# A Flamingo gated layer on one core: the query projection as three float32r products of high and low parts

## The reference

```python
h   = layernorm(x)
Q   = heads(h   @ Wq.T + bq)          # 16 heads of 16
K,V = heads(ctx @ Wk.T + bk), heads(ctx @ Wv.T + bv)
E   = where(mask == 0, -1e10, Q K^T / sqrt(16))
x   = x + tanh(g_xattn) * (softmax(E) V @ Wfc.T + bfc)
g   = layernorm(x) @ gate             # 8 experts, the best 2 with softmax weights
x   = x + tanh(g_ffn) * sum over the 2 of  w * ((silu(h w0_e) * (h w1_e)) wo_e)
```

## Time and profile before

| what | us |
|---|---|
| median of 3 runs | 1440.11 |
| lowest and highest run | 1439.74, 1444.11 |
| the profiled execution, span | 1441.3 |
| attention stage in it, about | 0 to 740 |
| expert stage in it, about | 750 to 1441 |

### The profile page before, as it was taken

How to read it: one execution, slowest core, us unless ns; L and a number is a source line. 1 busy time by engine, 2 the same in 40 slices (tenths; PEclk the granted TensorE clock), 3 DMA queues, 4 the chain that set the end, 5 groups by cost and what they waited for, 6 DMA issues and landing times.

```text
span 1441.3 us, 35541 instructions
## 1 busy us (share of the span) xinstructions
PE 1340.0 (93%) x9634; PEld 1173.3 (81%) x9635; DVE 808.2 (56%) x2519; ACT 697.4 (48%) x1779; POOL 895.5 (62%) x1389
## 2 busy tenths in 40 slices
PE   3999999999999999999939999999999999999996
PEld 3898888888888888888827788888888888888885
DVE  3688788888788888888643333333333333333332
ACT  2566566566566566566513333333333333333332
POOL 3478888888888888888853344444444444444443
PEclk9999999999999999999959999999999999999998
DMA  5033313333313333313677784333333333333332
GB/s 148 18 112 120 119 58 108 123 118 115 117 61 108 123 118 115 117 61 108 205 209 211 200 220 80 54 51 55 54 51 58 52 51 54 55 51 52 58 52 38
DMA packets 73811, 139.70 MB, mean 97 GB/s; under 512 B 11568, under 2 KB 54992, under 8 KB 71600
## 3 DMA queue, kind: packets, MB, share of 16 engines
q0 software_dynamic: 32064, 52.46, 18.5%
q1 hardware_dynamic: 39696, 84.87, 18.2%
q10 hardware_dynamic: 2016, 1.93, 0.5%
HBM read 68.95 MB, written 70.27 MB: 97 GB/s over the span
## 4 chain that ended last, share of the span: by engine, by line
PE 53%; issue 13%; POOL 11%; DVE 10%; DMA 6%; ACT 5%; POOLq 1%; DVEq 1%; ACTq 0%; SPq 0%; another core or an unknown queue 0%
PE banks L1296 23%; PE psB L1315 12%; PE banks L1137 4%; PE psT L1304 3%; DMA out_dram<-ey,eid 3%; POOL routed_rows L478 2%; DMA et<-routed_rows 2%; PE psG L1281 2%; ACT prob L604 2%; PE psT L1149 2%; PE banks L1089 2%; ACT prob L608 2%; DVE qT L809 2%; PE psB L1161 1%; POOL rs L421 1%
## 5 line engine op out<-in xcount | busy, mean ns | idle before, releaser
L531 POOL DMA_INDIRECT out_dram<-ey,eid x135 | 217.3, 1609 | 374.8 <-issue 141.0
L1296 PE MATMUL banks<-w_all,etT 128*128 x1620 | 434.2, 403 | 0.7 <-ACT etT L715 0.7
L1038 DVE TENSOR_TENSOR hgT<-psT,hgT 128x512 fp32r<-128x512 f32 x135 | 93.4, 692 | 430.4 <-ACT hgT L727 430.4
L1296 PEld LDWEIGHTS banks<-w_all,etT 128*128 128x128 f32 x1620 | 287.0, 190 | 51.4 <-issue 3.4
L1315 PEld LDWEIGHTS psB<-w_all,hgT 128*128 128x128 f32 x1620 | 208.1, 188 | 17.9 <-issue 1.3
L1315 PE MATMUL psB<-w_all,hgT 128*128 x1620 | 216.9, 283 | 0.8 <-ACT hgT L727 0.8
L733 ACT ACTIVATE ey<-psB,ewt 128x256 f32<-128x256 f32 x135 | 64.1, 475 | 240.4 <-DMA out_dram<-ey,eid 180.1
L721 ACT ACTIVATE hs<-banks 128x512 f32<-128x512 f32 x135 | 80.7, 598 | 186.1 <-PE psT L1304 181.5
L432 POOL TENSOR_TENSOR kbd<-kT,own 128x616 fp32r<-128x616 f32 x128 | 152.4, 1222 | 24.3 <-DVE kT L831 24.3
L1161 PE MATMUL psB<-vbd,probT 128*128 128x51 f32 x1280 | 160.0, 273 | 0.0
L1161 PEld LDWEIGHTS psB<-vbd,probT 128*128 128x128 f32 x1280 | 157.2, 194 | 1.6
(11 more groups left out here) (159 smaller groups left out, 2309.3 us busy)
## 6 DMA issues: line engine op xcount, KB each, us to landing
split_weights<-w_part SPq DMA_DIRECT2D x16, 1536.0 KB
w_all<-split_weights SPq DMA_DIRECT2D x32, 768.0 KB
et<-routed_rows POOLq DMA_DIRECT2D x135, 129.0 KB, 3.3
xb<-in_x_dram SPq DMA_DIRECT2D x32, 256.0 KB, 2.8
w_raw<-in_L_ffn_w_kernel_dram SPq DMA_DIRECT2D x32, 256.0 KB
out_dram<-x SPq DMA_DIRECT2D x64, 128.0 KB
w_raw<-in_L_ffn_wo_kernel_dram SPq DMA_DIRECT2D x16, 256.0 KB
cb<-in_ctx_dram SPq DMA_DIRECT2D x32, 77.0 KB
```

The source lines that it names most:

```text
L531: gp.indirect_dma_start(out=out, out_offset=bass.IndirectOffsetOnAxis(ap=eid[:, u:u + 1], axis=0), in_=ey[:, u % 2, :], in_offset=None, co ...
L1296: m = pe.matmul(banks4[:, bank], etT[:, u % 2, a, c], weight(e, c, w, n), start=(j == 0), stop=(j == len(steps) - 1))
```

## The change

Both operands of the query projection are held as a high and a low part in float32r. The two high parts are what ACT's copies write (of the weights once, of x in each batch); the two low parts are new subtractions on DVE, `psum - high`: one for the weights at the start, and `x_low(b)` for each batch, 128 x 512 elements each. `queries` then makes three products of parts (high x high, low weights x high x, high weights x low x) in float32r where there was one in float32. PE waits for the low part of x (`xT_lo`) ahead of each `queries`, and for that of the weights (`wq_lo`) before it does anything behind the weights' transposes.

```diff
--- before.py
+++ after.py
@@ -100,7 +100,7 @@
         sb("early_weights", [P, EARLY * 2 * QW])
         w_raw = sb("w_raw", [P, FR, F])
         w_part = sb("w_part", [P, 2, FR, F], F32R)
-        wT = {n: sb(f"{n}T", [P, DC, D]) for n in ("wk", "wq", "wv", "wfc")}
+        wT = {n: sb(f"{n}T", [P, DC, D]) for n in ("wk", "wv", "wfc")}
         gate_sb = sb("gate_sb", [P, DC, E])
         bias = sb("bias", [P, 3, DC])
         bfc_rows = sb("bfc_rows", [P, D])
@@ -134,7 +134,8 @@
         xg = sb("xg", [P, 2, QT, D])
         cb = sb("cb", [K2, 2, D])
         xn = sb("xn", [P, QT, D])
-        xnT = sb("xnT", [P, DC, S])
+        xnT = sb("xnT", [P, 2, DC, S], F32R)
+        wqT = sb("wqT", [P, 2, DC, D], F32R)
         ctxT = sb("ctxT", [P, DC, K2])
         vparts = sb("vparts", [K2, 3, D], BF16)
         vrest = sb("vrest", [K2, D])
@@ -221,7 +222,7 @@
         x1_out, pad_out, scattered = [sem("x1_out0"), sem("x1_out1")], sem("pad_out"), [sem(f"scattered{j}") for j in range(4)]
 
         iota_done, ident_done, dv_const = sem("iota_done"), sem("ident_done"), sem("dv_const")
-        wT_ps, wT_sb, tanh_done, valid_done = sem("wT_ps"), sem("wT_sb"), sem("tanh_done"), sem("valid_done")
+        wT_ps, wT_sb, wq_lo, xT_lo, tanh_done, valid_done = sem("wT_ps"), sem("wT_sb"), sem("wq_lo"), sem("xT_lo"), sem("tanh_done"), sem("valid_done")
 
         stat1, mvar1, eps1, rstd1, xn_done = sem("stat1"), sem("mvar1"), sem("eps1"), sem("rstd1"), sem("xn_done")
         xg_done, kbd_done, mrow_done = sem("xg_done"), sem("kbd_done"), sem("mrow_done")
@@ -564,9 +565,10 @@
                         act.dma_start(bias[:, n, a:a + 1], v[a * P:(a + 1) * P].rearrange("(q o) -> q o", o=1)).then_inc(const_in, 16)
             act.wait_ge(gates_in, 32)
             act.activation(tanhg[:], gates[:], ACT.Tanh).then_inc(tanh_done, 1)
-            for n, name in enumerate(wT):
+            for n, name in enumerate(("wk", "wq", "wv", "wfc")):
                 act.wait_ge(wT_ps, n + 1)
-                act.copy(wT[name][:].rearrange("p c d -> p (c d)"), banks4[:, n]).then_inc(wT_sb, 1)
+                dst = wqT[:, 0] if name == "wq" else wT[name][:]
+                act.copy(dst.rearrange("p c d -> p (c d)"), banks4[:, n]).then_inc(wT_sb, 1)
             act.wait_ge(const_in, 16 * CONST_LOADS)
 
             def ctx_evac(b):
@@ -584,7 +586,7 @@
 
             def x_evac(b):
                 act.wait_ge(xT_ps, b + 1)
-                act.copy(xnT[:].rearrange("p c s -> p (c s)"), psA[:]).then_inc(xT_sb, 1)
+                act.copy(xnT[:, 0].rearrange("p c s -> p (c s)"), psA[:]).then_inc(xT_sb, 1)
 
             def q_evac(b, u):
                 act.wait_ge(q_ps, b + 1)
@@ -808,6 +810,11 @@
 
                 return dve.scalar_tensor_tensor(out=dst, in0=ps_part, scalar=bias_part, in1=high.bitcast(F32), op0=ALU.add, op1=ALU.subtract)
 
+            def x_low(b):
+                dve.wait_ge(xT_sb, b + 1)
+                dve.tensor_tensor(xnT[:, 1].rearrange("p c s -> p (c s)"), psA[:], xnT[:, 0].rearrange("p c s -> p (c s)").bitcast(F32),
+                                  ALU.subtract).then_inc(xT_lo, 1)
+
             def q_low(b, u):
                 dve.wait_ge(q_sb, DC * (b + 1))
                 for a in range(DC):
@@ -925,6 +932,10 @@
                 dve.tensor_copy(slot[:, u4], slotf[:]).then_inc(slot_done, 1)
                 dve.wait_ge(base_done, i + 1)
 
+            dve.wait_ge(wT_sb, 2)
+            dve.tensor_tensor(wqT[:, 1].rearrange("p c d -> p (c d)"), banks4[:, 1], wqT[:, 0].rearrange("p c d -> p (c d)").bitcast(F32),
+                              ALU.subtract).then_inc(wq_lo, 1)
+            x_low(0)
             k_evac(0)
             k_split(0, 0)
             k_split(0, 1)
@@ -937,6 +948,7 @@
             s_negate(0, 0)
             s_shift(0, 0)
             k_evac(1)
+            x_low(1)
             k_split(1, 0)
             k_split(1, 1)
 
@@ -986,6 +998,8 @@
                         place(i - 3, (u4 - 3) % 4)
                     if known(i, 2):
                         choose(i - 2)
+                    if t == 1 and more2:
+                        x_low(b + 2)
 
             batches(dve, batch)
             free_rows(NT - 3, 0)
@@ -1101,8 +1115,10 @@
             def queries(b, a):
 
                 pe.wait_ge(xT_sb, b + 1)
-                for c in range(DC):
-                    m = pe.matmul(psA[:, a * S:(a + 1) * S], wT["wq"][:, c, a * P:(a + 1) * P], xnT[:, c], start=(c == 0), stop=(c == DC - 1))
+                pe.wait_ge(xT_lo, b + 1)
+                for j, (w, x_part) in enumerate(((0, 0), (1, 0), (0, 1))):
+                    for c in range(DC):
+                        m = pe.matmul(psA[:, a * S:(a + 1) * S], wqT[:, w, c, a * P:(a + 1) * P], xnT[:, x_part, c], start=(j + c == 0), stop=(j + c == DC + 1))
                 if a == DC - 1:
                     m.then_inc(q_ps, 1)
 
@@ -1197,6 +1213,7 @@
                 pe.matmul(psG[:, D + 2 * E:D + 3 * E], ones[:], chosen_any[:], start=True, stop=True).then_inc(r_ps, 1)
 
             pe.wait_ge(wT_sb, 4)
+            pe.wait_ge(wq_lo, 1)
             ctx_T(0, 0, 0)
             x_T(0)
             keys(0)
```

## The result

The changed kernel took 1451.21 us (median of 20 runs, 1445.60 to 1456.97), the kernel before 1444.87 in the same 20 rounds (1438.10 to 1451.04): a ratio of 1.0037, with a 95% interval from 1.0022 to 1.0052 (the two medians by themselves stand at 1.0044). On the 1440.11 us of the earlier runs the ratio gives 1445.4, or +5.3 us (3.2 to 7.5), where +4.2 was forecast. So it is slower, by little, but clear of no change. In the experiments one run of e1, of 1896.44 us at a granted clock of 0.65, is a slow one and is left out of its ratio.

A forecast was written before the change was run, and what follows sets the result against it. Bound: a 21.6 us loop per batch through POOL, ACT, PE and DVE, not PE. Start +3.9, clock +0.8, first batches -0.5, steady part 0: +4.2 us, a median of 1444.3 us, range 1437.0 to 1451.0.

The forecast's parts named there:

- The ring: Steady attention loop: dependencies through POOL, ACT, PE and DVE set the pace, 21.63 us a batch; query projection lies outside.
- nothing from PE's saving: Query products in the steady batches: 0.27 us a batch spared on PE, counted 0 because PE just waits longer.
- Low part of x, 0: New DVE subtraction each batch, 0.692 us, fits in DVE's wait ahead of the keys' evacuation; counted 0.
- rival B: Low part of x comes too late on DVE: 0.12 us a batch, +3.4 us, 1447.7 (1464 if dear); chance 0.12.
- The start, +3.9: Program start: PE waits for the weights' low part to about 24.3 us, so the first queries end 3.9 us later.
- the 0.5 us counted: First batches: queries of batches 1 and 2 lie on the way, so 2 x 0.27 = 0.5 us comes back.
- The clock, -1.6 to +1.8: TensorE's clock after the start: 1.2 GHz costs up to +1.8, scores may regain 1.6; booked at +0.8 us.
- Steady part, 0: Attention batches after the first ones: neither cheaper products nor the low part of x changes the time; counted 0.
- Rival A: PE is the bound after all: 31 batches save 0.27 us each, 8.4 us, giving 1436.4 us; chance 0.16.
- C: Start delay shrinks from 3.9 to 2 us through the clock in early scores, 1440.5; sign: under 2 us later; chance 0.10.

The follow-up runs named there:

- e1: Kernel before, plus the low part of the query weights made on DVE at the start and waited for by PE, but not used; ratio to before 1.0023.
- e3: Changed kernel with the high x high product alone, the low parts still made and waited for; ratio to before 1.0062.
- e7: Changed kernel with early low parts at the start, DVE's bf16 cast moved to ACT, and PE's keys ahead of probability transposes and scores; ratio to before 0.9917.
- e12: Kernel before (one float32 product) with DVE's bf16 cast moved to ACT and PE's keys ahead of probability transposes and scores; ratio to before 0.9920.
- e4: Changed kernel with the subtraction for the low part of x done twice in each batch from batch 2 on; ratio to before 1.0081.
- e10: Kernel before with the one edit that DVE's bf16 cast is done by ACT; ratio to before 0.9978.
- e11: Changed kernel, its start left as is, with the one edit that DVE's bf16 cast is done by ACT; ratio to before 1.0002.
- e9: Kernel before run again unchanged for a second profile; span 1448.8 us.
- e2: Changed kernel with the low parts of the query weights and of x(0) made earlier, PE waiting only ahead of its first queries; ratio to before 1.0043.
- e5: Changed kernel run again unchanged for one more profile; span 1448.0 us.

## Why the prediction was right, point by point

- *The ring, and nothing from PE's saving.* Right, and shown three ways: the turn is 21.59, e3 with eight products fewer is no faster, and e7 and e12 turn alike. PE's two waits grew by some 0.3 us a batch together (7.8 and 0.2 us in 85 to 700), where 0.27 was expected. A run of six products takes 0.95 us (less 0.28 for the last, over five: 0.134 each, where the sum had 0.123).
- *Low part of x, 0.* Right: 683 ns at the median, DVE's wait for the keys shorter by 0.59 and still there. e4 shows where it would have cost (rival B): a second one did. The price of B, 0.12 us a batch, had only the lateness in it; in e4 the lateness costs 0.2 in one of two batches, and the operation of POOL that DVE's cast then falls on another 0.4.
- *The start, +3.9.* PE idle to 23.85 (24.3 expected), first queries ending at 29.54 (28 to 30 expected), 5.3 us behind before; the values behind them start 5.3 us later too (31.38 for 26.12). Then this shrank by more than the 0.5 us counted. PE in the scores of batch 0, before (beside 32.42 in the earlier trace rows) and after:

```profile
39.98 1.12 PE L1149 MATMUL psT<-ident,prob 128*128 128x128 f32 x4 [2.30 <-ACT prob L608]
...
44.41 0.60 PE L1149 MATMUL psT<-ident,prob 128*128 128x128 f32 x4
```

```profile
37.05 3.25 PE L1153 MATMUL banks<-kbd,qT 128*128 128x462 f32 x12
...
44.12 0.66 PE L1165 MATMUL psT<-ident,prob 128*128 128x128 f32 x4 [2.54 <-ACT prob L610]
...
46.98 0.60 PE L1165 MATMUL psT<-ident,prob 128*128 128x128 f32 x4
```

  The scores start 4.6 us later, the transposes behind them 4.1, the next ones 2.6. The last two steps are the clock: before had 1.2 GHz from 29.7 to 36.5 and from 40.0 to 43.4, after 2.4 GHz from 39.6 on. The step before them, 0.6, is mostly one subtraction of DVE for the values, which took 1.33 us (L843) before and 0.83 (L850) after. `kbd` of batches 1 and 2, before and after, and DVE's low part of x for batch 1:

```profile
40.11 4.77 POOL L432 TENSOR_TENSOR kbd<-kT,own 128x616 fp32r<-128x616 f32 x4 [8.69 <-DVE kT L831]
64.61 4.76 POOL L432 TENSOR_TENSOR kbd<-kT,own 128x616 fp32r<-128x616 f32 x4 [2.28 <-DVE kT L831]
```

```profile
45.92 4.77 POOL L433 TENSOR_TENSOR kbd<-kT,own 128x616 fp32r<-128x616 f32 x4 [11.22 <-DVE kT L838]
66.88 4.76 POOL L433 TENSOR_TENSOR kbd<-kT,own 128x616 fp32r<-128x616 f32 x4 [2.29 <-DVE kT L838]
```

```profile
44.58 0.69 DVE L815 TENSOR_TENSOR xnT<-psA,xnT 128x512 fp32r<-128x512 f32 x1 [1.10 <-ACT xnT L589]
```

  +5.8 and +2.3 us, and +2.0 for batch 3. Of the 5.8, 1.6 is that low part, which stands between two steps of the keys and waits for ACT: e1 has none, and its K(1) is 44.31, while its PE is at the same place as that of after (44.18 and 44.12). By batch 2 nothing is left of it, as the prediction said. From there e1 and after show the three products alone: K(2) is 67.22 and 66.88, 0.34 us back, where 0.5 was counted. So the net +4.2 was too large for this pair: it measured +2.3 at K(2), +2.0 at K(3) and, with turns shorter by 0.03 us, +1.3 at K(31). Between e10 and e11 it was 3.5 by the ratios, and 5.3 in K(2), with the clock of e11 against it.
- *The clock, -1.6 to +1.8.* Both sides came. Up to the end of the first queries 1.2 GHz cost 1.8 us, as counted (twelve products took 2.85 us, 2.9 expected); in the scores it gave 2.1 back, which the prediction had called luck and booked at half. The net was -0.3 and not +0.8. The whole start in these terms is then 3.9 - 0.45 (PE goes on at 23.85) + 1.8 - 2.1 - 0.6 (DVE) - 0.3 (products) = +2.3, which is K(2). And the bounds took the clock of before as fixed, which it is not. One kernel, twice: K(2) of before at 64.61 and, in e9, at 67.41, where the clock first rose at 27.1 us instead of 19.5. That is 2.8 us without any change. PE in e9, against the earlier trace rows:

```profile
21.90 1.83 PE L1089 MATMUL banks<-ctxT,wkT 128*128 128x77 f32 x8
23.53 3.70 PE L1105 MATMUL psA<-xnT,wqT 128*128 128x256 f32 x8
```

  The same queries take 3.70 us, not 1.98, in the same program. After and e11, alike but for who makes the cast: 66.88 and 70.15, the first rise at 19.1 and at 30.1.
- *Missing from the sum: the long turn.* "Steady part, 0" holds for the short turn alone. The long one costs 0.16 us a batch in before and 0.21 in after, 4 to 6 us in all, as much as the whole forecast. Of the plain profiles one of two is long in either kernel. Whether the change makes it more frequent is not settled: e2 and e3, which have the low parts of x, are long in most batches and e1, which has none, is short, but after and before have one profile of either sort, and one profile tells no share. So of the measured +5.3 us, the start is shown to cost (e1: 0.7 to 6 us; 2 to 3.5 by the other measures); the remaining 2 to 3 may be the long turn or nothing. That +4.2 came as close as it did is in part luck: its own term, the start, was smaller in the pair of profiles, and something the sum did not hold, or noise, made up for it.
- *Rival A* is dead. *B* did not happen. *C* was half right: the delay did shrink to about 2 us, by the clock in the scores of batch 0, and its sign (less than 2 us) is just met or just missed. Its price doesn't follow from the sum, though: 1.9 us off 1444.3 is 1442.4, not 1440.5.

## What to carry to other kernels

Before pricing a cheaper instruction, follow one turn of the loop around the engines; an engine 95% busy can still be outside the ring, and then its saving turns into its own wait. Where the ring passes through POOL, look at what DVE runs within a tenth of a microsecond of POOL's small instructions: here a cast that started 0.03 us behind one cost nothing and 0.04 ahead of it 0.2 us a turn, and the same program did both. Giving the cast to ACT ended it. Take two profiles of the same kernel before explaining a difference of 0.3%.

## What the runs showed of the hardware

- Two turns of one loop in the same program, 21.59 us (after) and 21.80 (e5), each held from batch 5 to the end, told apart by the order of two instructions that start 0.03 to 0.04 us apart.
- TensorE's clock first rose at 18.4 to 19.8 us in ten of the fourteen profiles, about where the sixteen transposes end, and at 27.0 (e7), 27.1 (e9), 30.1 (e11) and 41.3 (e4) in the others, with the same transposes ahead. For one program this moved K(2) by 2.8 us (before, e9).
- The expert stage, the same code in all, took 687.0 to 697.2 us: on a single profile this hides a change of 0.5%.
- float32r products of 256 columns follow each other at 0.134 us in the attention stage and at 0.123 in the expert stage.
